# Expert weights in one run per partition and deeper buffers in the expert stage of a fused attention and mixture kernel

## The reference, cut to what matters

```python
E, K, F = (64, 8, 192)
C = 128                                   # slots of an expert
probs = softmax(x @ router_w.T)           # x: 8192 tokens x 256
topk_w, topk_ids = top_k(probs, K)        # weights scaled to sum 1
...
x_buf = zeros((E * C + 1, 256)).at[idx].set(x[tok])   # a token without a slot is dropped
g = einsum('ecd,edf->ecf', xb, w_gate)
u = einsum('ecd,edf->ecf', xb, w_up)
h = silu(g) * u
y = einsum('ecf,efd->ecd', h, w_down)
routed = segment_sum(y[safe] * flat_w, tok)
out = x + routed + shared(x)
```

## Time and profile before

| | |
|---|---|
| median of 3 runs | 3040.85 us (3040.02 to 3042.74) |
| profiled execution, whole | 3049.17 us |
| its span | 3047.4 us |
| mean granted TensorE clock | 0.959 |
| busy in the span: TensorE, VectorE, ScalarE, GpSimd | 90%, 72%, 34%, 27% |
| DMA: bytes moved, mean rate | 327.31 MB, 107 GB/s |
| chain that ended last: DMA out<-x_mem,sidx (combine) | 1.3% of the span |
| transfers of gate, of up, of down | 192 KB each |

### The profile page before, as it was taken

One profiled execution on the slowest core, in us unless ns is written; L12 is line 12 of the kernel. 1 busy time (PEld: TensorE's weight loads), 2 busy tenths in 40 slices (PEclk: granted clock), 3 DMA queues, 4 the chain that ended last, 5 costly groups with the idle time before them and its releaser, 6 DMA issues. The chain is left out here.

```text
span 3047.4 us, 61516 instructions
## 1 busy us (share of the span) xinstructions
PE 2749.3 (90%) x23816; PEld 2290.7 (75%) x23816; DVE 2206.7 (72%) x5944; ACT 1039.7 (34%) x1524; POOL 819.8 (27%) x858
## 2 busy tenths in 40 slices
PE   2599999999999999999999999999999999865787
PEld 1388888888888888888888888888888888635676
DVE  2467888888887888878888888888878887632333
ACT  1223333333333333333333333333333333211111
POOL 1000122222222222222222222222222222334333
PEclk7599999999999999999999999999999999958999
DMA  6623343343333333333333333333323331116897
GB/s 192 181 86 100 113 125 112 111 115 109 107 103 91 91 96 99 99 99 92 84 96 99 89 99 94 93 99 98 91 78 97 99 92 40 55 24 167 199 221 164
DMA packets 352927, 327.31 MB, mean 107 GB/s; under 512 B 46429, under 2 KB 348311, under 8 KB 352636
## 3 DMA queue, kind: packets, MB, share of 16 engines
q1 hardware_dynamic: 318844, 304.21, 35.6%
q0 software_dynamic: 33792, 19.17, 3.7%
HBM read 182.18 MB, written 212.37 MB: 129 GB/s over the span
## 5 line engine op out<-in xcount | busy, mean ns | idle before, releaser
L642 ACT ACTIVATE exps<-second 128x1024 f32<-128x1024 f32 x512 | 525.6, 1027 | 784.1 <-PE second L1124 769.7
L537 POOL DMA_INDIRECT expert_slots<-row,sidx x512 | 508.6, 993 | 794.8 <-PE first L1106 554.2
L1204 PE MATMUL mixp<-w_h,r_part_h 128*128 128x256 f32 x3072 | 670.0, 299 | 39.7 <-DVE hid L895 23.8
L811 DVE TENSOR_REDUCE nm<-first 128x4 f32<-128x1024 f32 x512 | 623.5, 1218 | 95.1 <-PE first L1106 95.0
L1204 PE MATMUL mixp<-w_h,r_part_l 128*128 128x256 f32 x3072 | 610.7, 280 | 0.0
L1204 PE MATMUL mixp<-w_l,r_part_h 128*128 128x256 f32 x3072 | 610.0, 280 | 0.0
L1204 PEld LDWEIGHTS mixp<-w_h,r_part_h 128*128 128x128 f32 x3072 | 468.4, 189 | 97.6 <-DVE hid L895 33.6
L1204 PEld LDWEIGHTS mixp<-w_l,r_part_h 128*128 128x128 f32 x3072 | 469.2, 188 | 0.0
L1204 PEld LDWEIGHTS mixp<-w_h,r_part_l 128*128 128x128 f32 x3072 | 469.1, 188 | 0.0
L895 DVE SCALAR_TENSOR_TENSOR x_mem<-mixp,C,x_mem 128x256 f32<-128x256 f32 x768 | 329.9, 477 | 118.0 <-PE mixp L1204 116.7
L895 DVE SCALAR_TENSOR_TENSOR hid<-mixp,C,hid 128x256 f32<-128x256 f32 x704 | 301.0, 475 | 36.6 <-PE mixp L1204 34.6
(11 more groups left out here) (203 smaller groups left out, 3577.2 us busy)
## 6 DMA issues: line engine op xcount, KB each, us to landing
kst<-k_parts SPq DMA_DIRECT2D x256, 192.0 KB
qst<-q_parts SPq DMA_DIRECT2D x256, 192.0 KB
q_parts<-nat_h SPq DMA_DIRECT2D x128, 256.0 KB
k_parts<-ctx_part_h SPq DMA_DIRECT2D x64, 256.0 KB, 2.4
k_parts<-nat_h SPq DMA_DIRECT2D x64, 256.0 KB, 2.4
q_parts<-nat_l SPq DMA_DIRECT2D x64, 256.0 KB
exps<-in_wg SPq DMA_DIRECT2D x64, 192.0 KB
exps<-in_wu SPq DMA_DIRECT2D x64, 192.0 KB
```

The costliest lines, as they stand in the source:

```text
L537: pool.e.indirect_dma_start(out=slots_dram, out_offset=bass.IndirectOffsetOnAxis(ap=sidx[b % 2][:, t, k:k + 1], axis=0), in_=row[b % 2][:, ...
L642: act.e.activation(exps[:, j % NU, :, :, :].rearrange("p k t s -> p (k t s)"), second[:, :, :].rearrange("p k s -> p (k s)"), ACT.Exp, sca ...
L811: dve.e.tensor_reduce(nm[u % 2][:, :, 2 * j:2 * j + 2].rearrange("p t k -> p k t"), first[:, :, :].rearrange("p k (t s) -> p k t s", t=TIL ...
L1204: m = pe.e.matmul(mixp[q % 2][:, t * D:(t + 1) * D], src[i][:, dt, t * P:(t + 1) * P], wmix[n][j][:, l, dt, :], start=(k == 0), stop=(k == ...
```

## The change

- Gate and up weights are stacked on the host and laid out as expert, partition, (gate or up, half, column), so that one transfer loads both and each partition's share is one run of 3072 B. Before, each was a transfer of 256 runs of 768 B. Down is laid out likewise: 96 runs of 2048 B in the place of 192 of 1024 B.
- NW goes from 3 to 5, NX from 4 to 8, NY from 4 to 6. Row numbers have a count of their own, NID = 8 in the place of 4. The memory is taken from buffers that the earlier stages are done with: `row` (now one tensor, `row_mem`), two of the five x buffers, `ctx_o`, the first v buffer, all three q buffers.
- SyncE waits for the end of what used that memory, and loads experts 3 and 4 between the third and the fourth of the first eight row loads.
- VectorE's `e_same` of pair p waits for adds up to pair p-4, and `e_down` for adds up to pair p-3. GpSimd's waits stay as they were.

```diff
-        row = [sb(f"row{i}", (P, TILES, ROW)) for i in range(2)]
+        row_mem = sb("row_mem", (P, 2, TILES, ROW))
+        row = [row_mem[:, i] for i in range(2)]
...
-        NW, NX, NY = 3, 4, 4
+        NW, NX, NY, NID = 5, 8, 6, 8
         WGU = 2 * DT * FH
-        ewgu = [exps_flat[:, i * WGU:(i + 1) * WGU].rearrange("p (u a f) -> p u a f", u=2, a=DT) for i in range(NW)]
-        down_mem = [exps_flat[0:FC, NW * WGU + i * 2 * D:NW * WGU + (i + 1) * 2 * D].rearrange("p (a d) -> p a d", a=2)
-                    for i in range(NW)]
+        gate_flat = [exps_flat[:, i * WGU:(i + 1) * WGU] for i in range(3)]
+        gate_flat += [t[:, :, :, :].rearrange("p i t n -> p (i t n)")[:, 0:WGU] for t in (row_mem, x_mem[:, NY // 2:NXB])]
+        ewgu = [t.rearrange("p (u a f) -> p u a f", u=2, a=DT) for t in gate_flat]
+        down_flat = [exps_flat[:, 3 * WGU + i * 2 * D:3 * WGU + (i + 1) * 2 * D] for i in range(3)]
+        down_flat += [ctx_o[:, :, :].rearrange("p t d -> p (t d)"), v_x[0][:, :, :, :].rearrange("p t h r -> p (t h r)")]
+        down_mem = [t[0:FC, 0:2 * D].rearrange("p (a d) -> p a d", a=2) for t in down_flat]
         erow = [t[:, :, :].rearrange("p n s -> p (n s)")[:, i * ROW:(i + 1) * ROW].bitcast(F32)
-                for t in q_st[0:2] for i in range(2)]
-        eid = [sidx[0][:, 0, i:i + 1] for i in range(NX)]
+                for t in q_st for i in range(3)][0:NX]
+        eid = [sidx[0][:, 0, i:i + 1] for i in range(NID)]
...
-        ey = [X[i][:, 0, :] for i in range(NY)]
+        ey = [X[i // 2][:, i % 2, :] for i in range(NY)]
...
-                        for n in range(NW):
-                            for u, w in enumerate((wg_in, wu_in)):
-                                sp.e.dma_start(ewgu[n][:, u], w[n].rearrange("(a p) f -> p a f", p=P)).then_inc(
-                                    c_gu[n], 16)
-                            sp.e.dma_start(down_mem[n], wd_in[n].rearrange("(a p) d -> p a d", p=FC)).then_inc(
-                                c_down[n], 16)
+
+                        def load_expert(n):
+                            sp.e.dma_start(ewgu[n], wgu_in[n]).then_inc(c_gu[n], 16)
+                            sp.e.dma_start(down_mem[n], wd_in[n]).then_inc(c_down[n], 16)
+
+                        for n in range(3):
+                            load_expert(n)
+                        sp.wait_ge(v_co, HALVES)
+                        sp.wait_ge(p_xc, NB)
+                        sp.wait_ge(a_out, HALVES)
+                        sp.wait_ge(t_out, HALVES)
                         for s_ in c_scat:
                             sp.wait_ge(s_, 128 * NB)
                         for n in range(NX):
                             sp.e.dma_start(erow[n], slots_dram[n * CAP:(n + 1) * CAP, :]).then_inc(c_er[n], 16)
+                            if n == 2:
+                                for s_ in c_out:
+                                    sp.wait_ge(s_, 16 * (NB // 2))
+                                load_expert(3)
+                                load_expert(4)
...
                         sp.wait_ge(t_eg, e - NW + 1)
-                        for u, w in enumerate((wg_in, wu_in)):
-                            sp.e.dma_start(ewgu[e % NW][:, u], w[e].rearrange("(a p) f -> p a f", p=P)).then_inc(
-                                c_gu[e % NW], 16)
+                        sp.e.dma_start(ewgu[e % NW], wgu_in[e]).then_inc(c_gu[e % NW], 16)
...
-                        sp.e.dma_start(down_mem[e % NW], wd_in[e].rearrange("(a p) d -> p a d", p=FC)).then_inc(
-                            c_down[e % NW], 16)
+                        sp.e.dma_start(down_mem[e % NW], wd_in[e]).then_inc(c_down[e % NW], 16)
...
-                            out=out_pad, out_offset=bass.IndirectOffsetOnAxis(ap=eid[e % NX], axis=0), in_=ey[e % NY],
+                            out=out_pad, out_offset=bass.IndirectOffsetOnAxis(ap=eid[e % NID], axis=0), in_=ey[e % NY],
...
-                    dve.wait_ge(c_add, 32 * max(0, pair - 1))
-                    dve.e.tensor_copy(eid[high % NX], high_no).then_inc(v_id, 1)
+                    dve.wait_ge(c_add, 32 * max(0, pair - NID // 2 + 1))
+                    dve.e.tensor_copy(eid[high % NID], high_no).then_inc(v_id, 1)
...
-                    pe.wait_ge(c_gu[e % NW], 32 * (e // NW + 1))
+                    pe.wait_ge(c_gu[e % NW], 16 * (e // NW + 1))
...
+    def expert_rows(w, p):
+
+        w = w.reshape(w.shape[:-2] + (w.shape[-2] // p, p, w.shape[-1]))
+        return np.ascontiguousarray(np.moveaxis(w, -2, 1))
...
-        "wg": a["L1_ffn_w_gate"],
-        "wu": a["L1_ffn_w_up"],
-        "wd": a["L1_ffn_w_down"],
+        "wgu": expert_rows(np.stack([a["L1_ffn_w_gate"], a["L1_ffn_w_up"]], 1), P),
+        "wd": expert_rows(a["L1_ffn_w_down"], fc),
```

More of the change, by code:

```diff
@@ L112, in build @@
 def build(nc, x_in, ctx_in, ctxT_in, wqT_in, wkvT_in, woT_in, qk_cols_in, bv_cols_in, bo_in, pw_in, uT_in,
-          w1T_in, w2T_in, b2_in, rT_in, wg_in, wu_in, wd_in, wsgu_in, wsd_in, out_pad):
+          w1T_in, w2T_in, b2_in, rT_in, wgu_in, wd_in, wsgu_in, wsd_in, out_pad):
     NB, S, D = x_in.shape
@@ L125, in build @@
     CAP = 128
-    FH = wg_in.shape[2]
+    FH = wgu_in.shape[4]
     FC = FH // 2
@@ L994, in vector_program @@
                     dve.wait_ge(v_seq, seq.n)
-                    dve.e.scalar_tensor_tensor(eid[low % NX], id_step, id_flag, low_no, ALU.mult, ALU.add).then_inc(v_id, 1)
+                    dve.e.scalar_tensor_tensor(eid[low % NID], id_step, id_flag, low_no, ALU.mult, ALU.add).then_inc(v_id, 1)
                 elif what == "e_gate":
```

## The result

The changed kernel takes 3033.35 us (median; 3023.01 to 3036.98), the kernel before 3042.74 us in the runs beside it. The ratio is 0.9965, 95% interval 0.9954 to 0.9976: faster by 7 to 14 us. I had forecast 3006.8 us and a range up to 3033.0. The sign was right, the size was not: of the 34.1 us that I had worked out, 9.4 came by the medians.

What follows compares the result with a forecast made beforehand. GpSimd's serial scatter turn per expert pair was taken as the bound: 1.85 + 5.65 = 7.50 us, 1.10 less over 31 turns, 34.1 us off the 3040.85 us median, giving 3006.8 us; range 2980 to 3033.

Steps and rivals of the forecast that it cites:

- The loop: In the experts' stage, GpSimd's combine takes one serial turn per expert pair, waiting for the high add's landing: 8.60 us a turn.
- Term one: Low to high scatter start: more result and row-number buffers have both results ready, 2.65 to 1.85 us, 0.80 us a turn.
- High start to the next low start: High add behind weight loads: earlier load burst, mostly given back by later loads, leaves 0.3 us net, 5.95 to 5.65.
- The layout, a relief inside the 0.3: Weight loads in longer runs: 0.16 to 0.58 us less DMA work a pair, counted inside the 0.3 us net gain.
- Rival (C): Longer load packets hold up the adds' rows: 0.8 us an add, 0.8 us a turn slower net, 3066 us; chance 0.08.
- More buffers for weights and rows: Deeper weight and row buffers only let TensorE run ahead until the adds hold it; nothing gained on GpSimd's loop.
- Rival (B): High add meets more loads after the shorter gap: 6.6 us, turn 8.45, 5 us less in all, 3036 us; chance 0.14.
- (A): High add finds an empty queue, TensorE then bounds the turn at 6.7 us: 59 us less, 2982; chance 0.16 with near cases.
- Two rules on the DMA engines: Skill page: runs of 512 B already reach line rate, so layout worth nothing; engines switch queues only at packet ends.
- signs of failure: In the expert turns: high start to next low above 6.5 us, or TensorE's gate and down filling all of a turn.
- signs of success: High 1.85 us after low, next low near 5.6 later, GpSimd waiting on its own landings, DMA share near 0.86, TensorE's row waits nearly gone.

Runs made afterwards that it cites:

- paced kernel: The changed kernel with each pair's loads held until GpSimd marks adds three pairs back as sent, row loads two experts later: 3006.39 us, 0.9867 of the kernel before.
- held kernel: The changed kernel with each pair's loads grouped, row loads two experts later, all held for the landing of adds: 3047.56 us, 0.9985 of the kernel before.

## Why the prediction was wrong, point by point

- **The loop.** Right. GpSimd's turn per pair, closed by the landing of the high add, sets the stage; it held in every kernel.
- **Term one, 2.65 to 1.85 us from low to high.** Right in mechanism: 1.85 in 28 of 31 turns. Two turns with 5.2 and 7.3 us, present in all kernels, and the first with 3.3 make the mean 2.17, so 0.5 came of 0.8. I took the last pair's gap for the mean of all. The mean before, 2.65, had the same late turns in it (4.4, 5.2 and 3.3), which the buffers don't remove.
- **High start to the next low start, 5.95 to 5.65 us.** This is the step that failed, with the sign: it became 6.23. I reckoned how much earlier the loads would be ahead of the high add, and forgot that the low add lies between. The load burst did move from 2.4 us after the landing to 0.5 us, as worked out; but there its packets run among those of the low add and of the high one, 5.5 us for the two in the turn above, while before the low add's had gone by nearly alone. So the move was a cost where I had booked 0.3 us of relief. That the release at the landing is what costs, the paced and the held kernel show. The two crowded rows that I had the earlier trace rows already said that a gap made shorter comes back as a longer wait; I gave that 0.14.
- **The layout, a relief inside the 0.3.** Wrong sign. Alone it costs 0.46 us a turn, 9 to 20 us in all. Rival (C) priced it at 1.6 us for both adds, or 0.8 for one; the direction was right for the layout alone, the size about half of one; as a forecast of the whole change (slower, 3066) it did not come. Its mechanism, a row waiting for each long packet, is not shown: the two halves of the layout cost about equally little and neither is clear of the other.
- **More buffers for weights and rows.** "None of this is on GpSimd's loop" was right for the crowded turns and missed where they pay: they let the last load go 31 us ahead of the last scatter and not 13, and six turns at 6.74 are the whole gain of the profiled execution, 6 x 1.63 = 9.8 us less 25 x 0.15 = 3.8 us. But results and row numbers alone, with three weight buffers and loads that go on, gave the same total (7.0 to 8.2 us from the 26th turn on), so there are two ways to the same 12 us, the second not explained, and the parts don't add.
- **Rival (B), the crowd takes the gain,** is what happened in the crowded turns. That its total is so near, 3036 against 3033, is luck in part: it had 1.85 and 6.6 us in every turn, where the means are 2.17 and 6.22, and no short turns at the end. At 0.14 it was far too little, since my own reading of the trace had the DMA share at 0.81 and crowded turns in the majority. **(A)** needed the loads out of the adds' way; the paced kernel goes towards it, at 3006 and not 2982.
- **Two rules on the DMA engines.** By the rule on runs of 512 B (the Trainium skill, "DMA: Bandwidth & Descriptors", Specifications) the layout would be worth nothing; here it was worth less than nothing alone. The same page of the Trainium skill, section on queues, rings and completion order, lets engines go round packet by packet. The window 2880.2:2882.3 above, with loads alone, has no bearing on it, since an add's packets come some 2 us after its start in an emptier queue too. In 2882.3:2885.3 both queues move side by side, 67.8% and 40.6%, which agrees with taking turns; the order of single packets can't be seen.
- **What I had named as signs of failure** fitted in half the turns: high to next low is above 6.5 us in 16 of 31, with a mean of 6.22. Of the signs of success the gap came, and TensorE waits at the shared part (L1328, L1317 before) and after the first expert no longer for rows; but GpSimd's wait is still put down to L997 (L986 before), and the DMA share is 0.77 where I had 0.86.

## What to carry to other kernels

When a serial chain of small transfers shares the DMA engines with bulk loads, ask of every buffer that is added which event now releases the loads. If it is the end of the chain's own link, loads and link start together, the link's packets crawl among theirs, and the engines idle at the turn. Holding the loads for the moment when the link had been sent let the same traffic fit beside it here. The engines' mean share (0.77) says nothing of this: look at one turn in slices, and at what goes out in the first microsecond after the gate opens.

## What the runs showed that I had not expected

- In every kernel here the high scatter of the eighth and of the twenty-third turn comes late, 4.4 to 7.3 us after low, where with the deeper buffers its neighbours have 1.9. These are 15 turns, 30 scatters, apart, and GpSimd's idle time there is, in most kernels, put down to the landing of its own transfers. What recurs every 30 scatters was not tried.
- The same code can run in turns of about 7.6 or of about 9.1 us within one execution (one transfer, short runs); that the phase of loads and adds is the cause is not shown. A difference of 0.2% between two such kernels says little on what an instruction costs.
- A weight load's bytes are free or dear by their place: 1.18 MB a pair cost 1.5 us a turn in the changed kernel and 0.6 us in the paced one (7.45 against 6.85), by one execution of each.
